# Window attention, conv mixer: score passes in two head halves with the relative bias in spare rows, key blocks placed by GpSimd's DMAs

## The chip, the cores and the metric

The kernel runs on one core of a Trainium2 chip, float32 in and out. The metric is the device time of one launch in microseconds (us), the median over several runs. A core has TensorE (PE, with its weight loads shown as PEld), VectorE (DVE), ScalarE (ACT), GpSimd (POOL) and SyncE (SP), which run side by side and meet at semaphores. PSUM is the memory that TensorE writes to.

## The reference, cut to what matters

Eight images of 64 channels and 32x32 pixels pass through an attention block with its MLP, and then through a block of gated depthwise convolutions. The change is in the attention block only. What that computes:

```python
xn = layernorm(xc)                       # over the 64 channels of each pixel
win = xn in windows of 8x8               # 64 tokens of 64 channels, 8 heads of depth 8
qkv = win @ w_qkv + b_qkv
attn = einsum('bnhd,bmhd->bhnm', q * 8 ** -0.5, k)
bias = rel_bias_table[REL_IDX.reshape(-1)].reshape(64, 64, 8)
attn = softmax(attn + bias.transpose(2, 0, 1)[None], axis=-1)
out = einsum('bhnm,bmhd->bnhd', attn, v) @ w_proj + b_proj
xc = xc + out
h = gelu(layernorm(xc) @ w_mlp1 + b_mlp1) @ w_mlp2 + b_mlp2
xc = xc + h
```

## The kernel before, in words

**Layout.** The 128 partitions hold two images at a time (a batch half `bh` of 64 channels each), and the columns hold four such pairs. The 4096 columns are worked off in NG = 8 groups of G = 512 columns. A group has NW = 8 windows of T = 64 tokens for each of its two images, and 8 heads.

**One window's scores.** A score matrix has 128 rows (64 keys of each of two images) and 512 columns (8 heads by 64 queries). All heads are had from one matrix product over 128 rows of contraction, because one of its two operands is block sparse. `q_heads` and `k_heads` have, for head h, only the rows of that head filled (every eighth row), and `k_blocks` and `q_blocks` have the two images on the diagonal. These operands are put in place by DMAs from `k_parts` and `q_parts`, with the unused places zeroed once at the start. The arithmetic is in float32r, a shortened float32, so the values are split in a high and a low part: for the true scores the product is taken three times (high by high, high by low, low by high).

**The passes.** For each window there is first a maximum pass, from high parts only (`scores_for_max`: one product and one more, `reverse` by `rel`, that adds the relative bias, both 512 columns wide), whose row maxima VectorE takes (`take_maximum`, line 1090). Once a group's eight windows have their maxima, TensorE transposes them (`transpose_maxima`) and VectorE spreads them negated into `minus_max`. The true score pass (`scores`) then has five products of 512 columns: three for the scores (line 778), one for the bias (780) and one, `pick` by `minus_max`, that takes the maximum off (781). ScalarE takes the exponentials (`exponentials`, line 544) into `probs`; TensorE multiplies by the values and by ones (`weighted_values`, `sums`), and VectorE divides (`divide_by_sums`).

**The order of the work.** Each engine has its own `step` for group g, written out by hand, and three later or earlier groups are worked on beside it: `nxt` = g+1 has its maximum pass, `far` = g+2 its layer norm, keys and queries, and `prev` = g-1 its projection, residual and second layer norm. TensorE's step is `scores` 0 to 4 with small work between them, `weighted_values` and `sums` of the first four windows, then the maximum passes in pairs between `scores` 5, 6 and 7, then `keys(far)`, `transpose_maxima(nxt)`, `queries(far)`, and `weighted_values` and `sums` of the other four. The steps of groups 2 to 3 run in a hardware loop on each engine, the others are written out. PSUM has three banks for the maximum pass and two for `scores`, so a maximum pass of window w waits for the reduction of window w-3, and `scores` of window w for the exponential of w-2.

**The waits around the change.** `keys(far)` waits until six of the eight reductions are done. On ScalarE the step ends with `evacuate_k`, `evacuate_q` and `high_of_x` of group g+3, which GpSimd waits for to make the low part (line 284, `low_of_x`), which TensorE waits for in `centered` of the next step. SP's queue holds all DMAs that place operands: `spread_keys` (8 DMAs to `k_heads`, one for each head) and, for each half of the windows, `spread_parts`, which first waits until `scores` of the group before no longer needs the place, then issues 2 DMAs to `k_blocks` and 8 to `q_heads`. GpSimd issues none.

**The start.** `split_bias` makes the bias operand `rel` on VectorE before the first group's `normalise`. GpSimd zeroes `q_blocks`, `k_blocks` and `q_heads`, VectorE `k_heads`.

## Time and profile before

| | us |
|---|---|
| median of 3 runs | 366.39 (365.82 to 370.71) |
| the profiled execution, its own time | 365.95 |
| its span in the trace | 364.1 |
| PE busy | 325.0 (89%) |
| PE weight loads busy | 224.4 (62%) |
| DVE busy | 231.9 (64%) |
| ACT busy | 215.5 (59%) |
| POOL busy | 71.4 (20%) |

The span is the time from the first to the last instruction; the time outside it is 1.85 us here. Busy times of PE are modelled from pipelined instructions: a 512 column product is shown as about 0.39 us long, while the next one starts 0.23 us after it, so starts are compared and not durations. In the chain that ended last, 76% is PE and 11% DVE. The attention steps lie between 36 and 209 us, the MLP after them to about 260, the convolutions to the end.

### The profile page before, as it was taken

The page shows a single profiled execution, that of the slowest core. Times are in us where ns is not written, and L with a number is a line of the kernel's source. Part 1 is how long each engine was busy: PE and PEld are TensorE (multiplying, and loading weights), DVE is VectorE, ACT ScalarE, POOL GpSimd, SP SyncE. Part 2 cuts the span into 40 slices and gives each one's busy share as a digit, 9 for nine tenths or more (in the row PEclk, how much of TensorE's full clock was granted, in tenths as well). Part 3 has the DMA queues.
Part 4 walks back from the last instruction along what each step waited for, and adds up shares of the span by engine and source line. Part 5 has one row for each costly group of instructions (what it writes and reads, how often), then busy time and mean ns, then how long its engine had stood idle before and what let it go on. Part 6 is the DMA issues. An engine that isn't in the chain of part 4 may idle for free.

```text
span 364.1 us, 6376 instructions
## 1 busy us (share of the span) xinstructions
PE 325.0 (89%) x2432; PEld 224.4 (62%) x2432; DVE 231.9 (64%) x376; ACT 215.5 (59%) x350; POOL 71.4 (20%) x63
## 2 busy tenths in 40 slices
PE   2567999999999999999998995999629999999994
PEld 1344676767767677676776753444127777777773
DVE  6557176386783866847758374446976799867411
ACT  6252826668476684765733587989586347646600
POOL 5371101212212122121020391123410000000000
PEclk9989999999999999999999998999959999999999
DMA  7523363322233212332132000076000657788721
GB/s 177 123 61 72 90 126 68 70 56 50 53 66 68 53 49 59 64 70 53 49 63 59 2 0 2 1 147 153 0 2 1 139 121 141 149 166 173 152 61 29
DMA packets 31147, 27.64 MB, mean 76 GB/s; under 512 B 21008, under 2 KB 27664, under 8 KB 31120
## 3 DMA queue, kind: packets, MB, share of 16 engines
q1 hardware_dynamic: 30544, 26.48, 34.6%
q10 hardware_dynamic: 576, 0.79, 0.8%
q8 instruction: 18, 0.29, 0.4%
q14 instruction: 9, 0.07, 0.1%
HBM read 3.78 MB, written 2.10 MB: 16 GB/s over the span
## 4 chain that ended last, share of the span: by engine, by line
PE 76%; DVE 11%; ACT 5%; DMA 3%; SPq 2%; issue 1%; POOL 1%; DVEq 0%; ACTq 0%
PE psum L1007 24%; PE psum L778 11%; PE psum L794 4%; PE psum L759 4%; PE psum L710 4%; PE psum L780 4%; PE psum L781 4%; PE psum L760 4%; PE psum L803 4%; DVE maxima L1090 3%; PE psum L923 3%; DMA probs<-in_rel_table 2%; PE psum L934 2%; PE psum L737 2%; PE psum L811 2%; PE psum L742 1%
## 5 line engine op out<-in xcount | busy, mean ns | idle before, releaser
L1007 PE MATMUL psum<-shifted,conv_w 128*128 128x512 f32 x336 | 87.4, 423 | 9.5 <-ACT conv_w L270 9.5
L1007 PEld LDWEIGHTS psum<-shifted,conv_w 128*128 128x128 f32 x336 | 65.0, 195 | 31.1 <-issue 10.3
L544 ACT ACTIVATE probs<-psum 128x512 f32<-128x512 f32 x64 | 38.3, 598 | 50.1 <-PE psum L781 49.3
L778 PE MATMUL psum<-q_heads,k_blocks 128*128 128x512 f32 x192 | 59.1, 416 | 0.0
L1090 DVE TENSOR_REDUCE maxima<-psum 128x8 f32<-128x512 f32 x64 | 41.1, 685 | 23.7 <-PE psum L760 23.7
L778 PEld LDWEIGHTS psum<-q_heads,k_blocks 128*128 128x128 f32 x192 | 34.9, 188 | 13.6 <-issue 7.1
L284 POOL TENSOR_TENSOR parts<-x,parts 128x256 fp32r<-128x256 f32 (+1 forms) x21 | 19.0, 919 | 102.1 <-ACT parts L493 57.2
L710 PE MATMUL psum<-parts,center_average 128*128 128x512 f32 x64 | 22.7, 438 | 13.7 <-DVE parts L284 12.5
L759 PE MATMUL psum<-k_heads,q_blocks 128*128 128x512 f32 x64 | 27.2, 425 | 4.7 <-DMA k_heads<-k_parts 3.3
L270 ACT CAST conv_w<-conv_w 32x896 fp32r<-32x896 f32 x32 | 30.0, 938 | 0.4
L1104 DVE RECIPROCAL inv_sum<-psum 128x256 f32<-128x256 f32 x16 | 28.0, 1749 | 3.3 <-PE psum L803 3.2
L284 POOL TENSOR_TENSOR parts<-square_logvar,parts 128x512 fp32r<-128x512 f32 x14 | 18.1, 1290 | 53.7 <-ACT square_logvar L557 27.4
L1314 DVE SCALAR_TENSOR_TENSOR x<-psum,weights,x 64x512 f32<-64x512 f32 x16 | 12.0, 750 | 23.3 <-PE psum L1007 23.1
L760 PE MATMUL psum<-rel,reverse 128*128 128x512 f32 x64 | 25.8, 403 | 0.0
L780 PE MATMUL psum<-rel,reverse 128*128 128x512 f32 x64 | 25.1, 393 | 0.0
L781 PE MATMUL psum<-minus_max,pick 128*128 128x512 f32 x64 | 25.0, 391 | 0.0
L662 ACT CAST conv_w<-whole_w 128x896 fp32r<-128x896 f32 x8 | 7.5, 941 | 27.6 <-DVE whole_w L1299 14.9
L710 PEld LDWEIGHTS psum<-parts,center_average 128*128 128x128 f32 x64 | 11.9, 204 | 18.8 <-issue 7.2
L794 PEld LDWEIGHTS psum<-probs,v_blocks 128*32 128x32 f32 x1024 | 15.0, 110 | 8.0 <-issue 8.0
L923 PE MATMUL psum<-normed,mlp_w 128*128 128x512 f32 (+1 forms) x64 | 19.9, 452 | 0.0
L759 PEld LDWEIGHTS psum<-k_heads,q_blocks 128*128 128x128 f32 x64 | 12.5, 196 | 11.4 <-issue 6.6
L630 ACT ACTIVATE hidden<-psum,mlp_bias 128x512 f32<-128x512 f32 x32 | 19.4, 698 | 0.0
(138 smaller groups left out, 516.6 us busy)
## 6 DMA issues: line engine op xcount, KB each, us to landing
shifted<-images SPq DMA_DIRECT2D x32, 332.5 KB, 5.5
k_blocks<-k_parts SPq DMA_DIRECT2D x32, 128.0 KB, 2.8
q_heads<-q_parts SPq DMA_DIRECT2D x128, 32.0 KB, 1.9
k_heads<-k_parts SPq DMA_DIRECT2D x64, 32.0 KB, 1.8
out<-x SPq DMA_DIRECT2D x8, 256.0 KB, 4.8
x<-in_x SPq DMA_DIRECT2D x6, 256.0 KB, 5.9
x<-in_x SPq DMA_DIRECT2D x4, 128.0 KB, 4.7
weights<-in_weights ACTq DMA_DIRECT2D x1, 443.0 KB, 7.9
```

The source lines that it names most:

```text
L270: ins = copy(conv_w[bh][shift * KS:(shift + 1) * KS, part, :, C:], w[(shift - 1) * KS:shift * KS, :, 0:C])
L284: return engine.tensor_tensor(low, whole, high.bitcast(F32), ALU.subtract)
L544: act.activation(probs[:, w, :], psum[:, PROB0 + w % 2, :], ACT.Exp).then_inc(S["ac_probs"], 1)
L710: ins = pe.matmul(psum[:, bank, :], center_average[:, which, :], parts[:, part, :], start=part == 0, stop=part == 1)
L759: pe.matmul(max_bank(w), q_blocks[:, w, :], k_heads[:, :, w * T:(w + 1) * T], start=True, stop=False)
L760: pe.matmul(max_bank(w), reverse[:], rel[:, 0, :], start=False, stop=True).then_inc(S["pe_max"], 1)
L778: pe.matmul(bank, k_blocks[:, w // (NW // 2), k_part, w % (NW // 2), :], q_heads[:, q_part, :, w * T:(w + 1) * T], start=k_part + q_part = ...
L780: pe.matmul(bank, reverse[:], rel[:, 1, :], start=False, stop=False)
L781: pe.matmul(bank, pick[:, w, :], minus_max[:, :, :], start=False, stop=True).then_inc(S["pe_scores"], 1)
L923: ins = pe.matmul(psum[:, HIDDEN0 + m, :], mlp1_w[:, part, f * 128:(f + 1) * 128], normed2[:, bh, bass.ds(n * G, G)], start=part == 0, sto ...
L1007: ins = pe.matmul(psum[:, CONV0 + bh, :], conv_w[bh][:, w_part, t, :], img[:, y:y + H - 1:2, x0:x0 + W], start=t == 0 and w_part + part == ...
L1090: dve.tensor_reduce(maxima[:, w * NH:(w + 1) * NH], max_bank(w).rearrange("p (h t) -> p h t", t=T), AX.X, ALU.max).then_inc(S["dv_max"], 1)
```

## The change: what it does

Heads are grouped in two halves of four, and the 64 channels are laid out so that the heads 0 to 3 of both images fill partitions 0 to 63 and the heads 4 to 7 partitions 64 to 127 (a new order of the weight columns on the host). A product for one head half then needs only 64 of the 128 rows. The other 64 rows carry the relative bias: on one side they hold the reversal matrix, on the other the bias of that head half, so that one product gives scores and bias. Each score product of 512 columns becomes two of 256, one for each head half, and the separate bias products are gone. `k_blocks` and `q_blocks` get one more dimension for the head half. The bias rows are written once, at the start, and the DMAs that place new keys and queries never touch them.

The first place is TensorE, between the end of the first `weighted_values` and `scores(g, 6)` of a step: maximum passes of windows 0 to 3, `scores(g, 5)` and `centered2`. Before:

```order
L759 MATMUL psum<-k_heads,q_blocks 128x512
L760 MATMUL psum<-rel,reverse 128x512
L778 MATMUL psum<-q_heads,k_blocks 128x512 x3
L780 MATMUL psum<-rel,reverse 128x512
L781 MATMUL psum<-minus_max,pick 128x512
```

and with the change:

```order
L823 MATMUL psum<-k_heads,q_blocks 128x256 x4
L842 MATMUL psum<-minus_max,pick 128x512
L845 MATMUL psum<-q_heads,k_blocks 128x256 x6
L823 MATMUL psum<-k_heads,q_blocks 128x256 x4
L773 MATMUL psum<-parts,center_average 128x512 x2
```

A window's maximum pass goes from two instructions of 512 columns to two of 256 (the rows of before show one window's pair, those of now two windows at a time), and a window's `scores` from five of 512 to one of 512 and six of 256.

The second place is the end of ScalarE's step. Before:

```order
L514 ACTIVATE k_parts<-psum,qkv_bias 128x2x256
L521 ACTIVATE q_parts<-psum,q_bias 128x2x256
L529 CAST q_blocks<-q_parts 64x8x64 x2
L493 CAST parts<-x 128x256 x2
```

and with the change:

```order
L561 ACTIVATE k_parts<-psum,qkv_bias 128x2x256
L568 ACTIVATE q_parts<-psum,q_bias 128x2x256
L577 CAST q_blocks<-q_parts 32x8x64 x4
L541 CAST parts<-x 128x256 x2
```

Each batch half was one copy of 64 partitions; each pair of head half and batch half is now one of 32 partitions and as many columns.

The third place is GpSimd's step, where the DMAs to `k_blocks` now stand:

```order
L285 TENSOR_TENSOR parts<-square_logvar,parts 128x512 [waits ac_sq]
L285 TENSOR_TENSOR parts<-x,parts 128x512 [waits ac_x1]
L285 TENSOR_TENSOR parts<-square_logvar,parts 128x512 [waits ac_sq2]
L450 DMA k_blocks<-k_parts 32x16x64 [waits dv_k_low,pe_scores]
L450 DMA k_blocks<-k_parts 32x16x64 x3
L285 TENSOR_TENSOR parts<-x,parts 128x256 [waits x_high]
```

Four DMAs, each for 32 partitions and both window halves, stand before the low part of x; they wait for all eight `scores` of the group before, and `scores(g, 0)` waits for all four of them.

The core of the diff:

```diff
         def _(pool):
+            def spread_key_blocks(n, par):
+                if isinstance(n, int) and n == 0:
+                    pool.wait_ge(S["k_blocks_zeroed"], 1)
+                    pool.wait_ge(S["k_blocks_set"], 1)
+                else:
+                    pool.wait_ge(S["pe_scores"], NW * n)
+                pool.wait_ge(S["dv_k_low"], n + 1)
+                for hh in range(2):
+                    for bh in range(2):
+                        r = slice(hh * 64 + bh * 32, hh * 64 + bh * 32 + 32)
+                        pool.dma_start(k_blocks[r, hh, :, :, :, bh * T:(bh + 1) * T]..., k_parts[r, par]...
+                                       ).then_inc(S["k_blocks_in"], 16)
...
+                if nxt is not None:
+                    spread_key_blocks(nxt, 1 - par)
                 if after is not None:
                     low_of_next_x(after)
+            pool.wait_ge(S["dv_rel_flipped"], 1)
+            pool.tensor_scalar(key_rows(0), bias_rows(rel_flipped, 0, range(NW)), not_in_half(0), None, ALU.mult)...
             low_of_next_x(1)
-            pool.memset(q_heads[:].bitcast(F32), 0.0).then_inc(S["zeroed"], 1)
+            spread_key_blocks(0, 0)
+            late = range(NW // 2, NW)
+            for half in range(2):
+                pool.tensor_scalar(query_rows(0, half, late), bias_rows(rel_high, half, late), not_in_half(half), None, ALU.mult)
             low_of_next_square(1)
+            for half in range(2):
+                ins = pool.tensor_scalar(query_rows(1, half, late), bias_rows(rel_low, half, late), not_in_half(half), None, ALU.mult)
             low_of_next_x(2)
...
         ScalarE, evacuate_q
-                for bh in range(2):
-                    r = slice(bh * C, (bh + 1) * C)
-                    ins = act.copy(q_blocks[r, :, bh * T:(bh + 1) * T]..., q_parts[r, par, :, 0, :]...)
+                for hh in range(2):
+                    for bh in range(2):
+                        r = slice(hh * 64 + bh * 32, hh * 64 + bh * 32 + 32)
+                        ins = act.copy(q_blocks[r, hh, :, bh * T:(bh + 1) * T]..., q_parts[r, par, :, 0, :]...)
         ScalarE, the start
+            for half in range(2):
+                ins = act.activation(k_blocks[:, half, :, 0], reversal()..., ACT.Copy, scale=not_in_half(half))
...
+            for half in range(2):
+                act.activation(query_rows(0, half, early), bias_rows(rel_high, half, early), ACT.Copy, scale=not_in_half(half))
             evacuate_k(0, 0)
             evacuate_q(0, 0)
+            for half in range(2):
+                ins = act.activation(query_rows(1, half, early), bias_rows(rel_low, half, early), ACT.Copy, scale=not_in_half(half))
...
         TensorE, scores_for_max and scores
-                pe.matmul(max_bank(w), q_blocks[:, w, :], k_heads[:, :, w * T:(w + 1) * T], start=True, stop=False)
-                pe.matmul(max_bank(w), reverse[:], rel[:, 0, :], start=False, stop=True).then_inc(S["pe_max"], 1)
+                for hh in range(2):
+                    ins = pe.matmul(max_bank(w)[:, hh * G // 2:(hh + 1) * G // 2], q_blocks[:, hh, w, :],
+                                    of_half(k_heads, hh)[:, :, w * T:(w + 1) * T], start=True, stop=True)
+                ins.then_inc(S["pe_max"], 1)
...
+                if w == 0:
+                    pe.wait_ge(S["k_blocks_in"], 64 * (g + 1))
...
-                for k_part, q_part in ((0, 0), (0, 1), (1, 0)):
-                    pe.matmul(bank, k_blocks[:, w // (NW // 2), k_part, w % (NW // 2), :], q_heads[:, q_part, :, w * T:(w + 1) * T], ...)
-                pe.matmul(bank, reverse[:], rel[:, 1, :], start=False, stop=False)
-                pe.matmul(bank, pick[:, w, :], minus_max[:, :, :], start=False, stop=True).then_inc(S["pe_scores"], 1)
+                pe.matmul(bank, pick[:, w, :], minus_max[:, :, :], start=True, stop=False)
+                for hh in range(2):
+                    for k_part, q_part in ((0, 0), (0, 1), (1, 0)):
+                        ins = pe.matmul(bank[:, hh * G // 2:(hh + 1) * G // 2], k_blocks[:, hh, w // (NW // 2), k_part, w % (NW // 2), :],
+                                        of_half(q_heads[:, q_part], hh)[:, :, w * T:(w + 1) * T], ...)
+                ins.then_inc(S["pe_scores"], 1)
...
         VectorE, the start
+            for half in range(2):
+                ins = dve.tensor_scalar(q_blocks[:, half], reversal(), not_in_half(half), None, ALU.mult)
...
-            split_bias()
+            bias_with_keys()
             normalise(0)
+            low_of_bias()
```

`bias_with_keys` copies the flipped bias table into `rel_flipped` (two copies of 64 partitions) and fills the bias rows of `k_heads` for one head half (2048 columns); `low_of_bias` makes `rel_low` with two subtractions. SP's `spread_parts` becomes `spread_queries`, with its 8 DMAs to `q_heads` alone, which for the first group wait for the bias rows (`q_heads_set0`, `q_heads_set1`).

## Rows read from the trace of the kernel before

**Rows 1.** The page: busy time of each engine, and clock granted to TensorE.

```profile
PE 325.0 (89%) x2432; PEld 224.4 (62%) x2432; DVE 231.9 (64%) x376; ACT 215.5 (59%) x350; POOL 71.4 (20%) x63
...
PEclk9989999999999999999999998999959999999999
```

**Rows 2.** Stretches of time: one whole step, the last but one, the last.

```profile
105.42:128.56 23.14, 23.08 (x242) 16.55 (x241) 15.88 (x26) 15.09 (x29) 5.28 (x5) 1.00 0.27 58
174.90:196.00 21.10, 20.19 (x233) 15.19 (x233) 13.99 (x23) 9.83 (x19) 2.58 (x2) 1.00 0.28 61
...
196.00:216.00 20.00, 19.72 (x223) 14.19 (x224) 11.98 (x15) 13.06 (x22) 9.56 (x8) 1.00 0.04 9
```

**Rows 3.** Timeline of PE: start, length, line, count, idle time before.

```profile
115.98 0.50 PE L759 MATMUL psum<-k_heads,q_blocks 128*128 128x512 f32 x1
...
120.44 0.39 PE L781 MATMUL psum<-minus_max,pick 128*128 128x512 f32 x1
120.67 0.39 PE L759 MATMUL psum<-k_heads,q_blocks 128*128 128x512 f32 x1
...
125.54 1.13 PE L737 MATMUL psum<-normed,qkv_w 128*128 128x512 f32 x2
126.59 1.10 PE L794 MATMUL psum<-probs,v_blocks 128*32 128x64 f32 x64
...
128.49 0.97 PE L778 MATMUL psum<-q_heads,k_blocks 128*128 128x512 f32 x3
...
129.75 1.05 PE L742 MATMUL psum<-qkv_w,normed 128*128 128x128 f32 x8
130.56 0.93 PE L778 MATMUL psum<-q_heads,k_blocks 128*128 128x512 f32 x3
...
131.80 0.62 PE L710 MATMUL psum<-parts,center_average 128*128 128x512 f32 x2
...
139.11 0.50 PE L759 MATMUL psum<-k_heads,q_blocks 128*128 128x512 f32 x1
```

**Rows 4.** All of one line and form: count, busy us, mean ns.

```profile
L778 PEld LDWEIGHTS psum<-q_heads,k_blocks 128*128 128x128 f32 x192 | 34.9, 188 | 13.6 <-issue 7.1 <-ACT probs L544 0.4
...
L406 POOL TENSOR_TENSOR pick<-consts 128x1024 fp32r<-128x1024 f32 x1 | 2.0, 2030 | 3.7 <-DMA consts<-in_consts 3.7
```

**Rows 5.** Timeline of DVE in the same step.

```profile
119.41 1.75 DVE L1104 RECIPROCAL inv_sum<-psum 128x256 f32<-128x256 f32 x1
...
121.53 1.88 DVE L1090 TENSOR_REDUCE maxima<-psum 128x8 f32<-128x512 f32 x3
123.83 1.29 DVE L1090 TENSOR_REDUCE maxima<-psum 128x8 f32<-128x512 f32 x2 [0.42 <-PE psum L760]
```

**Rows 6.** Timeline of ACT, the end of the step and the start of the next.

```profile
126.70 0.69 ACT L521 ACTIVATE q_parts<-psum,q_bias 128x512 fp32r<-128x512 f32 x1 [0.86 <-DMA q_heads<-q_parts]
127.42 1.25 ACT L529 CAST q_blocks<-q_parts 64x512 fp32r<-64x512 f32 x2
128.69 0.71 ACT L493 CAST parts<-x 128x256 fp32r<-128x256 f32 x2
```

**Rows 7.** Timeline of POOL, one step earlier.

```profile
106.35 1.41 POOL L284 TENSOR_TENSOR parts<-x,parts 128x256 fp32r<-128x256 f32 x2 [7.30 <-ACT parts L493]
110.93 1.29 POOL L284 TENSOR_TENSOR parts<-square_logvar,parts 128x512 fp32r<-128x512 f32 x1 [3.17 <-ACT square_logvar L499]
```

**Rows 8.** SP's queue over the end of that step; DMA issues of the page.

```profile
122.90 1.30 SPq L356 DMA_DIRECT2D k_blocks<-k_parts  x2
124.25 5.98 SPq L362 DMA_DIRECT2D q_heads<-q_parts  x8
...
k_blocks<-k_parts SPq DMA_DIRECT2D x32, 128.0 KB, 2.8
```

**Rows 9.** Timelines of the start: ACT, DVE and PE.

```profile
21.90 1.54 ACT L539 COPY v_blocks<-psum 64x256 f32<-64x256 f32 x4
23.46 0.60 ACT L498 ACTIVATE parts<-psum 128x512 fp32r<-128x512 f32 x1
...
30.82 0.69 DVE L1076 TENSOR_TENSOR normed<-psum,rstd 128x512 f32<-128x512 f32 x1 [1.15 <-ACT rstd L506]
...
35.97 1.03 PE L778 MATMUL psum<-q_heads,k_blocks 128*128 128x512 f32 x3
```

More of the change, by code:

```diff
@@ L303, in halves, with patches, of_half, not_in_half @@
             return t.rearrange("p (s c) -> p s c", s=2)
-        ZERO_Q_BLOCKS, ZERO_Q_HEADS, NZERO = 1, 4, 5
+        NZERO = 2
+        def patches(n):
+            return rel_raw[:, n, :, :].rearrange("p (a b) h -> p h a b", a=WS)[:, :, :, 0:WS]
+        def of_half(t, half):
+            return t[:, half * (NH // 2):(half + 1) * (NH // 2), :]
+        def not_in_half(half):
+            a = _AT["not_in_half"][0] + half
+            return consts[:, a:a + 1]
+        def reversal():
+            return const("reverse").unsqueeze(1).to_broadcast([128, NW, 128])
+        def bias_rows(rel, half, windows):
+            rel = of_half(rel.bitcast(F32).rearrange("p (h t) -> p h t", h=NH), half)
+            return rel.unsqueeze(2).to_broadcast([128, NH // 2, len(windows), T])
+        def key_rows(half):
+            return of_half(k_heads, half).rearrange("p h (w t) -> p h w t", t=T)
+        def query_rows(part, half, windows):
+            rows = of_half(q_heads[:, part], half).rearrange("p h (w t) -> p h w t", t=T)
+            return rows[:, :, windows.start:windows.stop, :]
         block = ctx.enter_context(nc.Block())
@@ L365, in _ @@
             spread_keys(0)
[L366 to L367 removed]
+            spread_queries(0, 0)
+            spread_queries(0, 1)
             spread_keys(1)
@@ L371, in _ @@
             for g in range(NG - 1):
-                for half in range(2):
-                    spread_parts(g + 1, half)
+                spread_queries(g + 1, 0)
+                spread_queries(g + 1, 1)
                 if g + 2 < NG:
@@ L401, in _ @@
         def _(pool):
-            for t in (q_blocks[:].bitcast(F32), k_blocks[:].bitcast(F32), gaps[:]):
-                pool.memset(t, 0.0).then_inc(S["zeroed"], 1)
+            pool.memset(k_blocks[:, :, :, 1].bitcast(F32).rearrange("p h s w t -> p (h s) (w t)"), 0.0).then_inc(S["k_blocks_zeroed"], 1)
+            pool.memset(gaps[:], 0.0).then_inc(S["zeroed"], 1)
             pool.wait_ge(S["consts_in"], 16)
@@ L603, in _ @@
             evacuate_q(0, 0)
+            act.wait_ge(S["dv_rel_low"], 1)
+            for half in range(2):
+                ins = act.activation(query_rows(1, half, early), bias_rows(rel_low, half, early), ACT.Copy, scale=not_in_half(half))
+            ins.then_inc(S["q_heads_set0"], 1)
             act.wait_ge(S["v_zeroed"], 1)
@@ L1039, in _ @@
             dve.tensor_scalar(qkv_w[:, 1:3, :], qkv_raw[:, 1:3, :], vec[:, 0:1], None, ALU.mult)
+            dve.wait_ge(S["consts_in"], 16)
+            for half in range(2):
+                ins = dve.tensor_scalar(q_blocks[:, half], reversal(), not_in_half(half), None, ALU.mult)
+            ins.then_inc(S["q_blocks_set"], 1)
             dve.wait_ge(S["pe_qkv_bias"], 1)
```

123 lines of the change are left out of this document (62 added, 61 removed).

## The prediction

> **What bounds the kernel now.** I read the page first. TensorE is busy for 89% of the span, nobody else for more than 64%, and its clock is at full speed (2.4 GHz) from the second slice to where attention ends [rows 1]. The stretches by step say more: in a whole attention step of 23.14 us TensorE is busy for 23.08, VectorE for 15.9, ScalarE for 15.1, GpSimd for 5.3 [rows 2]. So a step lasts as long as TensorE's instructions; counted back from group 6, which begins at 174.9, five such steps (groups 1 to 5) fill the time from 59 us on. The timeline of PE gives the price of one: a product of 512 columns takes 0.23 us from start to start (120.44 to 120.67) [rows 3]. The timelines of the other engines then show how far behind TensorE they are, which decides what a shorter TensorE step is worth.
>
> **TensorE's own share.** A step removes 16 instructions of 512 columns (8 in the maximum pass, 8 in `scores`), 3.7 us, and cuts the 32 other products with `k_heads`, `q_blocks`, `k_blocks` and `q_heads` from one of 512 to two of 256. Of the latter the trace has none in this form. Below half of 0.23 they can't be (0.114, as many columns in all); at the other end, if a weight load (0.188 us each [rows 4]) could not run under the product before it, it is 0.19. But the eight 128-column instructions of `values` take 0.81 us (129.75 to 130.56), 0.10 each, with a full 128x128 weight load before each [rows 3], so loads do run under products and keep that pace. I take 0.118. A window's `scores` then takes 0.23 + 6 x 0.118 = 0.94 us against 1.15, its maximum pass 0.24 against 0.46: per step 8 x 0.21 + 8 x 0.22 = 3.45 us less. If nothing else mattered, a step would last 19.7 us.
>
> **What is late next.** I walk one step of the changed kernel, with time 0 at its first maximum pass (115.98 in the trace, the next at 139.11 [rows 3]).
>
> 1. VectorE. Window 2's maximum pass comes after two others and one `scores`: 0.47 + 0.94 + 0.4 = 1.8 us. A reduction takes 0.61 (1.88 for three), `divide_by_sums` 2.12 (119.41 to 121.53) [rows 5]. So the third reduction ends at 2.45, the division at 4.57, and the other five at 7.7. In the kernel before, they end at 9.1 (125.12), with 0.42 us of idle time: VectorE is nearly the limit there already. TensorE, with three banks and `keys` waiting for the sixth reduction, loses about 0.9 us.
> 2. TensorE: transpose 0.36, `queries` 1.05 (125.54 to 126.59) [rows 3]: ends at 9.15, against 10.6 before.
> 3. ScalarE: `q_parts` 0.72, then the copies to `q_blocks`. Two took 1.25 [rows 6]. There are now four, and although each has half the partitions it has as many columns, so I keep 0.62 each: 2.5 us. `high_of_x` 0.71: ends at 13.2, against 13.4 before (129.40). Of the 1.4 us won so far only 0.2 are left.
> 4. GpSimd: low part of x, 1.41 [rows 7]: 14.7, and by the same sum 14.9 before.
> 5. TensorE's `centered` can start at 14.75. In the kernel before it starts at 15.8 (131.80) [rows 3], 0.9 after its data was there; now TensorE is through with the second values and sums (1.9, 126.59 to 128.49) at 11.05 and gets to `centered` two `scores` and the values later, at 11.05 + 0.94 + 0.81 + 0.94 = 13.75, and waits 1.0.
> 6. From there TensorE takes `centered` 0.46, `scores` 2 and 3 with the projection 2.7, a wait of about 0.25 for GpSimd's low square (1.29 [rows 7], after ScalarE's square, which stands behind an exponential and the four copies of v), variance 0.5, `scores` 4 0.94, values and sums 1.9: the step ends at 21.5.
>
> So **a step lasts 21.5 us** against 23.13: 1.6 of the 3.45 us are had, since the chain of reductions, queries, copies, low part and `centered` closes on itself. Five steps: 8.0 us.
>
> **Group 6** has no x to come. Its first part is TensorE's: 10.62 (128.49 to 139.11) less `centered` and variance (1.0) and 5 x 0.21, 8.6 us. The second part ends when `k_blocks` is there, 11.15 after its start (below). Together 19.7 against 21.1 [rows 2]: 1.4 less. **Group 7** has no maximum pass, and TensorE is busy throughout (19.72 of 20.0 us, the start of the MLP among them) [rows 2]: 8 x 0.21 = 1.7 less.
>
> **The start.** The bias rows cost VectorE two fills of `q_blocks`, GpSimd 2048 columns of `k_heads` and 4096 of `q_heads` in place of a memset of 8192, ScalarE two fills of `k_blocks` and four of `q_heads`. Most of it lies under waits for the first loads and for keys. What doesn't: between `q_parts` and `evacuate_v` ScalarE has two more copies (1.25) and two fills of 1024 columns, twice a 512-column instruction at 0.5 us from start to start. `evacuate_v` moves from 21.90 to 25.1, the square behind it from 23.46 to 26.7 [rows 9], and by way of GpSimd the `normalise` of group 1 from 30.82 to about 31.3: 0.5 us. In the first step the four copies stand before the first exponential, another 1.2; the shorter second part gives 1.0 back, and the passes of group 0 the rest. Net 0.25 later, with bounds of 0 and 4 (if GpSimd takes 2 us for each DMA, its low square is 4 us late).
>
> **GpSimd's DMAs.** SP took 0.65 us to issue one to `k_blocks` (1.30 for two), and 2.8 us from issue to landing [rows 8]. GpSimd issues none in this trace. From below I bound it by SP's 0.65; from above by the slowest instruction that GpSimd has in steady work, 2.03 us for 1024 columns [rows 4], about two columns for each 256-byte run of such a DMA. The nearest row in kind is SP's, the nearest in engine is the other, and I take 1.0. The four are issued once `scores(g, 7)` is done, at 5.0 in the walk, so the last lands at 5.0 + 4x + 2.15 = 7.15 + 4x us: 11.15 for x = 1.0. TensorE is ready for `scores(g+1, 0)` at 11.05, and 1.0 more cost nothing, because it then waits for x anyway. So in the five steps the DMAs are free up to x = 1.2. The cover is that wait: were `centered` ready earlier, they would be the limit. The queue behind them on GpSimd, the low part of x, is needed from 13.2 on, so it is held up only above x = 2.0. SP's queue gets 2.6 us a step shorter: after `scores(g, 7)` it has 5.98 for `q_heads` and, at that pace, no more for the 8 of `k_heads`, which with 2 us to land are there by 19, 2.5 us before they are needed. I cost that at nothing.
>
> The Trainium skill has a price (DMA: Bandwidth & Descriptors, Latency and other measured facts): the first byte of a DMA from GpSimd comes after about 1 us, from SP after 0.6. Added once to SP's pace, as an estimate, the last would land at 10.2 and the sum would stay; the same page (SWDGE vs HWDGE vs iDMA) says that GpSimd writes every descriptor in software, which speaks against this change, and no run here shows it yet.
>
> **Sum.** 365.95 + 0.25 - 8.0 - 1.4 - 1.7 = **355 us**. The profiled execution lies 0.4 below the median of 366.39, so the two can be held for one.
>
> **Rivals.**
>
> *A. GpSimd's DMAs become the limit (slower).* Place: `scores(g+1, 0)` waits for the last of four, where only the first half's two DMAs, issued four windows earlier, were waited for before. Each step is 7.15 + 4x - 12.05 longer, for groups 0 to 5, and the start of group 7's `scores`, with no wait for x behind it, slips by 7.15 + 4x - 11.15. It eats the whole gain at x = 1.6 (landing at 13.5), makes the kernel 2% slower at x = 1.85, and at the upper bound of 2.03 gives 355 + 6 x 3.2 + 4.1 = 378.5. For it: GpSimd takes 1.29 us where VectorE takes 0.69 for the same kind of work, and each DMA has 512 runs of 256 bytes. Against it: nothing of GpSimd's 15 idle us a step is needed for other work, and 512 KB is 3 to 4 us for the DMA engines, which are busy for 0.27 of the step [rows 2]. Chance 0.38 for x above 1.33, where the time is no longer 2% below: 0.14 for within 2%, 0.24 for slower.
>
> *B. TensorE stays the limit.* If the four copies are quicker for having half the partitions, or reductions overlap better, the chain falls under TensorE's 19.7 us. Then 5 x 1.8 = 9 less: 346. For it: TensorE's waits in my chain, 0.9 for reductions, 1.0 and 0.25 for GpSimd, are small sums of many rows. Against: each step of it is a measured row. Chance 0.10.
>
> *C. Pairs of 256 columns go at the pace of weight loads, 0.19.* `scores` takes 1.37, a maximum pass 0.38, a step 23.1 + 8 x 0.22 - 8 x 0.08 = 24.2, and the kernel 366 + 8 = 374. The row of `values` speaks against it. Chance 0.03.
>
> My forecast, 350 to 359, has 0.45, and 0.04 remains for a start that costs up to 4 us more (359 to 362). Two per cent, about what a measurement of this kernel can tell from no change, is 7.3 us: faster means below 359.1. That is the forecast and B, 0.55; within 2% 0.18; slower, A above x = 1.85 and C, 0.27. The range goes from B's 346 to A's upper bound of 379; the forecast's own is 350 to 359.
>
> **What the profile after would show.** First maximum pass to first maximum pass of 21.5 us in groups 2 to 5, with PE busy for about 19.7; products of 256 columns 0.12 apart; an idle time of PE before `centered`, ended by GpSimd's low part of x, of about 0.9 us, and before `keys` or the transpose, ended by a reduction; four copies to `q_blocks` of 0.62 each. If the idle time stands before `scores(g, 0)` and a DMA ended it, A holds, and the time from issue to landing gives x. If there is none before `centered`, B does. The forecast is wrong most of all if one DMA from GpSimd takes more than 1.3 us.

## The result, and the profile after

| | before | changed |
|---|---|---|
| median, us | 366.41 (365.82 to 370.71) | 373.37 (370.6 to 374.99) |
| ratio | | 1.0169 [1.0106, 1.0232] |
| profiled execution: its time, span | 365.95, 364.1 | 372.76, 371.0 |

The changed kernel is about 7 us slower where 11 us less were forecast; 373.4 lies in the range given. Whether it is more than 2% slower the interval leaves open, but not that it is slower. On another chip, on which both kernels were measured again, it was 372.55 against 369.97, a ratio of 1.0077 [1.004, 1.0113]. By these two ratios it costs 1 to 2%. They differ by the kernel before: its single executions took under 367 us in three of four on the first chip and in 2 of 44 on the others, where nearly all took 368 to 372.

From the page of the changed kernel (busy time, clock of TensorE, two DMA issues):

```profile
PE 311.6 (84%) x2560; PEld 222.4 (60%) x2560; DVE 237.4 (64%) x377; ACT 232.7 (63%) x374; POOL 102.1 (28%) x98
...
PEclk9966889999999999999987995999968999999999
...
k_blocks<-k_parts POOLq DMA_DIRECT2D x32, 128.0 KB, 4.1
...
k_heads<-k_parts SPq DMA_DIRECT2D x64, 32.0 KB, 1.8
```

Against [rows 1], TensorE has 13 us less to do and idles more; its granted clock is lower from 19 to 56 us and near 200 us. A DMA to `k_blocks` takes 4.1 us from issue to landing, where SP's, issued two at a time, took 2.8 [rows 8]. The waits of TensorE, by what ended them (total, times, longest):

```profile
PE psum L773 <- DVE parts L285: 15.2, 4, 5.9
...
PE psum L842 <- DMA k_blocks<-k_parts: 8.0, 7, 2.5
PE psum L823 <- DMA k_heads<-k_parts: 7.2, 1, 7.2
```

In the kernel before, the first kind came to 12.5 us, the second to nothing and the third to 3.3. To see when they cost time I cut both spans at the same events of PE's timelines (first `scores` of groups 1, 6 and 7, first product of the MLP, first of the convolutions). Microseconds of each stretch, and the forecast's term for it:

| stretch | before | changed | difference | forecast |
|---|---|---|---|---|
| to `scores(1, 0)` | 59.09 | 64.41 | +5.3 | +0.25 |
| five steps, to `scores(6, 0)` | 115.70 | 111.37 | -4.3 | -8.0 |
| to `scores(7, 0)` | 21.11 | 22.76 | +1.7 | -1.4 |
| to the MLP | 15.72 | 15.96 | +0.2 | -1.7 |
| to the convolutions | 59.22 | 62.95 | +3.7 | 0 |
| to the end | 93.3 | 93.5 | +0.2 | 0 |

No term of attention is right in full. One step of the changed kernel, from group 3's first maximum pass, on PE:

```profile
97.11 0.74 PE L823 MATMUL psum<-k_heads,q_blocks 128*128 128x256 f32 x4
...
105.30 1.12 PE L800 MATMUL psum<-normed,qkv_w 128*128 128x512 f32 x2
106.36 1.10 PE L860 MATMUL psum<-probs,v_blocks 128*32 128x64 f32 x64
...
108.96 0.47 PE L842 MATMUL psum<-minus_max,pick 128*128 128x512 f32 x1 [0.65 <-DMA k_blocks<-k_parts]
109.27 0.87 PE L845 MATMUL psum<-q_heads,k_blocks 128*128 128x256 f32 x6
109.98 1.05 PE L805 MATMUL psum<-qkv_w,normed 128*128 128x128 f32 x8
...
112.15 0.74 PE L773 MATMUL psum<-parts,center_average 128*128 128x512 f32 x2 [0.18 <-POOL parts L285]
...
119.13 0.62 PE L823 MATMUL psum<-k_heads,q_blocks 128*128 128x256 f32 x3
```

and ScalarE and GpSimd beside it:

```profile
107.18 2.50 ACT L577 CAST q_blocks<-q_parts 32x512 fp32r<-32x512 f32 x4
109.71 0.71 ACT L541 CAST parts<-x 128x256 fp32r<-128x256 f32 x2
```

```profile
102.41 2.57 POOL L450 DMA_DIRECT2D k_blocks<-k_parts  x4 [0.19 <-issue]
110.50 1.60 POOL L285 TENSOR_TENSOR parts<-x,parts 128x256 fp32r<-128x256 f32 x2 [5.52 <-ACT parts L541]
```

This is the walk of the prediction: queries done at 9.25 (forecast 9.15), high x at 13.3 (13.2), `centered` at 15.0 (14.75), six products of 256 columns in 0.71 us, 0.119 apart (0.118). Only the landing is off: GpSimd issues a DMA in 0.65 us, and `scores` can start at 11.85, where TensorE was ready at 11.2. In the next step it starts at 12.4, and the wait is 1.1. Of the four DMAs of a group the first lands 3.0 us after its issue and the last, the one that counts, 4.4 to 5.2.

### The profile page after: what moved, and what is told of

It is laid out like the page before. It is cut to its first block, busy times and chain, and to the rows that moved or that the text cites. A ratio compares the mean times of both kernels' runs of the same rounds, so it can differ in the third digit from the quotient of the medians.

```text
span 371.0 us, 6661 instructions
## 1 busy us (share of the span) xinstructions
PE 311.6 (84%) x2560; PEld 222.4 (60%) x2560; DVE 237.4 (64%) x377; ACT 232.7 (63%) x374; POOL 102.1 (28%) x98
## 2 busy tenths in 40 slices
DMA packets 15788, 27.66 MB, mean 75 GB/s; under 512 B 4624, under 2 KB 11280, under 8 KB 15760
## 3 DMA queue, kind: packets, MB, share of 16 engines
q1 hardware_dynamic: 13648, 22.29, 26.6%
q0 software_dynamic: 1536, 4.20, 6.9%
## 4 chain that ended last, share of the span: by engine, by line
PE 45%; POOL 13%; ACT 11%; issue 10%; DMA 9%; DVE 9%; SPq 1%; DVEq 0%; POOLq 0%; ACTq 0%
PE psum L1072 24%; DMA k_blocks<-k_parts 7%; POOL parts L285 6%; PE psum L845 5%; POOL k_blocks L450 4%; PE psum L988 3%; PE psum L773 3%; DMA x<-in_x 2%; PE psum L842 2%; PE psum L999 2%; ACT v_blocks L587 2%; DVE normed L1195 2%; POOL q_heads L472 2%; POOL q_heads L476 2%; ACT probs L592 1%
## 5 line engine op out<-in xcount | busy, mean ns | idle before, releaser
L845 PEld LDWEIGHTS psum<-q_heads,k_blocks 128*128 128x128 f32 x384 | 56.6, 196 | 5.6 <-issue 1.8
L845 PE MATMUL psum<-q_heads,k_blocks 128*128 128x256 f32 x384 | 57.7, 287 | 0.0
L773 PE MATMUL psum<-parts,center_average 128*128 128x512 f32 x64 | 25.2, 479 | 19.9 <-DVE parts L285 15.2
L842 PE MATMUL psum<-minus_max,pick 128*128 128x512 f32 x64 | 30.5, 477 | 9.6 <-DMA k_blocks<-k_parts 8.0
L823 PE MATMUL psum<-k_heads,q_blocks 128*128 128x256 f32 x128 | 24.1, 311 | 9.9 <-DMA k_heads<-k_parts 7.2
L823 PEld LDWEIGHTS psum<-k_heads,q_blocks 128*128 128x128 f32 x128 | 19.7, 204 | 15.3 <-issue 10.5
L1382 DVE SCALAR_TENSOR_TENSOR x<-psum,weights,x 64x512 f32<-64x512 f32 x16 | 12.0, 750 | 23.3 <-PE psum L1072 23.1
L450 POOL DMA_DIRECT2D k_blocks<-k_parts x32 | 20.8, 657 | 15.0 <-PE psum L845 8.9
L501 POOL TENSOR_TENSOR images<-square_logvar,images 128x512 f32 (+1 forms) x8 | 10.3, 1289 | 46.1 <-ACT images L707 46.1
L842 PEld LDWEIGHTS psum<-minus_max,pick 128*128 128x128 f32 x64 | 12.5, 195 | 17.2 <-issue 13.9
L577 ACT CAST q_blocks<-q_parts 32x512 fp32r<-32x512 f32 x32 | 19.7, 616 | 0.5
```

The source lines that it names most:

```text
L450: pool.dma_start(k_blocks[r, hh, :, :, :, bh * T:(bh + 1) * T].bitcast(F32).rearrange("p s l w t -> p (s l w) t"), k_parts[r, par].bitcast ...
L773: ins = pe.matmul(psum[:, bank, :], center_average[:, which, :], parts[:, part, :], start=part == 0, stop=part == 1)
L823: ins = pe.matmul(max_bank(w)[:, hh * G // 2:(hh + 1) * G // 2], q_blocks[:, hh, w, :], of_half(k_heads, hh)[:, :, w * T:(w + 1) * T], sta ...
L842: pe.matmul(bank, pick[:, w, :], minus_max[:, :, :], start=True, stop=False)
L845: ins = pe.matmul(bank[:, hh * G // 2:(hh + 1) * G // 2], k_blocks[:, hh, w // (NW // 2), k_part, w % (NW // 2), :], of_half(q_heads[:, q_ ...
```

## The experiments

Each ratio is to runs of the kernel before on the same chip. Its medians there were 370.0 to 370.5 us, 4 us above the 366.4 of the first chip, so ratios are compared, and times only between traces. Dots mark what is left out of a diff; semaphore counts that an edit makes necessary are left out too.

**SP issues the key blocks** (all 32, between the two query halves).

```diff
 GpSimd, step
-                if nxt is not None:
-                    spread_key_blocks(nxt, 1 - par)
 SP, for each group
                 spread_queries(g + 1, 0)
+                spread_key_blocks(g + 1, (g + 1) % 2)
                 spread_queries(g + 1, 1)
```

> The changed kernel, with the DMAs to k_blocks issued by SP again (four a group, between the two halves of the queries' DMAs, after the same wait), nothing else changed. Theory A (GpSimd's DMAs cost time in every step and in the last one): SP's issue takes 0.65 us like GpSimd's, but they land 2.8 us after issue and not 4.1, so the wait for k_blocks before scores(g, 0), 0.65 to 1.2 us a step in the changed kernel, goes, and the 2.5 us before group 7 with its gap of 4.15 us in front of the 32nd DMA go too: steps of about 21.8 us for 22.3, s(7) 3 us earlier, and the kernel about 367 to 368. Theory B (the loss is at the start and the chain through ScalarE and GpSimd closes at 22 us anyway): steps stay at 22.0 to 22.3 and the kernel above 370.

364.01 us (363.42 to 364.27), ratio 0.9811 [0.9764, 0.9859], 3 us under what either theory gave. This undoes one of the change's two parts, and the other is a gain. By stretch: 63.05, 108.95, 19.79, 14.45, 62.42, 93.3. Of the 9.0 us less than the changed kernel's span, 2.4 are in the five steps, 3.0 in group 6, 1.5 in group 7, 1.4 in the start. In the steps, what ends TensorE's waits now is what the walk named, and the blocks are waited for once, ahead of group 7:

```profile
PE psum L773 <- POOL parts L285: 7.1, 14, 1.1
...
PE psum L842 <- DMA k_blocks<-k_parts: 0.6, 1, 0.6
```

**Group 0's blocks from SP, the other 28 from GpSimd.**

```diff
 GpSimd, start
-            spread_key_blocks(0, 0)
 SP, start
             spread_keys(0)
+            spread_key_blocks(0, 0)
             spread_queries(0, 0)
```

> The changed kernel with group 0's four key-block DMAs issued by SP and the other 28 by GpSimd. Theory of the shared start: in the changed kernel the k_heads DMAs took 3.3 us to land beside GpSimd's k_blocks DMAs (1.8 before), so the first max pass began at 27.66 instead of 25.44; here it begins near 25.7, as when SP issued all blocks (25.65). Theory of a full ring: GpSimd's 32nd DMA stalled 4.15 us because of how many it had issued; with 28 there is no such stall, and group 7's first scores come about 11.5 us after its max pass begins instead of 14.2. Together the time is 2 to 5 us under the changed kernel's 373.4. Rival: the stall belongs to that place in the program (GpSimd held by something else near 190 us) and stays at 4 us whatever the count; and the late start comes from the fills on GpSimd, so the first max pass stays at 27.7. Then the time is within 1 us of 373.4.

369.18 us (365.61 to 372.07), ratio 0.9946 [0.9903, 0.9989]. Both theories, of the shared start and of the full ring, hold in what they said of the trace. In the changed kernel the first key DMAs share the time from 19 to 25 us with GpSimd's, and the issues in the stretch from 17 to 30 us (count, size, us to landing) read

```profile
k_blocks<-k_parts POOLq DMA_DIRECT2D x4, 128.0 KB, 4.1
k_heads<-k_parts SPq DMA_DIRECT2D x8, 32.0 KB, 3.3
```

and in this one

```profile
k_blocks<-k_parts SPq DMA_DIRECT2D x4, 128.0 KB, 3.3
k_heads<-k_parts SPq DMA_DIRECT2D x8, 32.0 KB, 1.8
```

so its first maximum pass starts at 25.89 instead of 27.66 (25.44 before). The second view also gives SP's price for four of these DMAs in a row, 3.3 us and not the 2.8 of two; the page of the version with x first, below, has 3.3 as well. And GpSimd isn't held in group 6. The changed kernel's GpSimd there:

```profile
189.61 1.93 POOL L450 DMA_DIRECT2D k_blocks<-k_parts  x3 [0.19 <-issue]
195.69 0.66 POOL L450 DMA_DIRECT2D k_blocks<-k_parts  x1 [4.15 <-issue]
```

this one's:

```profile
189.07 2.58 POOL L466 DMA_DIRECT2D k_blocks<-k_parts  x4 [0.18 <-issue]
```

The five steps stay at 111.1. And of the 1.8 us won at the first maximum pass only 0.3 are left at `scores(1, 0)` (64.11), which now waits 2.2 us for group 1's blocks: GpSimd issued them from 55.52 on, and the last landed at 63.9, 6.2 us after its issue. Why so long there, no run tells.

**Four more DMAs** (group 1's issued a second time, 36 in all; one run).

```diff
 GpSimd, step, after spread_key_blocks(nxt, 1 - par)
+                    if isinstance(nxt, int) and nxt == 1:
+                        pool.wait_ge(S["k_blocks_in"], 128)
+                        spread_key_blocks(nxt, 1 - par)
```

> The changed kernel with the four key-block DMAs of group 1 issued a second time by GpSimd (the same data to the same place), 36 in all instead of 32. Theory of a full ring: what holds GpSimd is the count of its DMAs, so the hold of 4 us moves one group forward, ahead of the fourth DMA of group 6 (near 172 us, the 32nd issued), and the fourth of group 7 has none or one of its own. Rival: it belongs to group 7's place in the program, and stays ahead of the fourth DMA of group 7 alone, near 196 us. In both the first scores of group 1 come some 4 us later.

383.12 us, one run, with `scores(1, 0)` at 71.23. The hold moved one group forward, with its count:

```profile
155.25 2.57 POOL L450 DMA_DIRECT2D k_blocks<-k_parts  x4 [0.18 <-issue]
177.43 1.93 POOL L450 DMA_DIRECT2D k_blocks<-k_parts  x3 [0.19 <-issue]
183.56 0.66 POOL L450 DMA_DIRECT2D k_blocks<-k_parts  x1 [4.19 <-issue]
201.75 2.57 POOL L450 DMA_DIRECT2D k_blocks<-k_parts  x4 [0.21 <-issue]
```

28 DMAs stand ahead of the group at 177.43, so the held one is again the 32nd. It is the count, not the place. The traces also show when the hold ends: the 31st DMA lands at 182.88 and GpSimd issues the 32nd at 183.56; in the changed kernel it lands at 195.01 and the issue is at 195.69. So GpSimd seems to wait here until its earlier DMAs have landed. What it is that is full after 31 such DMAs is not shown.

**The kernel before with GpSimd issuing its key blocks** (after all eight `scores`, as in the changed kernel).

```diff
 SP, spread_parts
-                    sp.dma_start(k_blocks[r, half, ...
 GpSimd, step
+                if nxt is not None:
+                    spread_key_blocks(nxt, 1 - par)
```

> The kernel before, with only the DMAs to k_blocks moved to GpSimd: its four DMAs of a group are issued after all eight scores of the group before, where SP had issued the first half's two after four of them. Scores in one piece, bias products kept. Theory A: in the kernel before, 5.7 us lie between the last scores of a group and the first of the next; four issues of 0.65 and 4.1 us to land from the last one take 6.1, so each step waits 0.5 to 1 us, the 32nd DMA is held up as in the changed kernel (2 us more before group 7), and the kernel takes 370 to 374. Theory B: the DMAs from GpSimd are slow only beside the changed kernel's other DMAs: steps stay at 23.1 and the kernel at 366 to 368.

370.86 us (368.86 to 373.46), ratio 1.0043 [1.0, 1.0086]. The wait in each step that theory A named did not come. With the long score passes the DMAs hide: TensorE waits for `k_blocks` once, 0.5 us, and the five steps take 115.9. The page has 3.7 us to landing, and the 32nd DMA is held there too (3.03 us, until 0.01 us after the 31st landed). So in the five steps the same move costs next to nothing where a step is 23.1 us long, and 2.4 us where it could be 21.8.

The trace is 4.2 us longer than that of the kernel before, and 3.5 of them lie in the stretch from the MLP to the convolutions (62.73 for 59.22), which this edit doesn't touch. The next run is about that stretch.

**Memsets later.** When the last scores are done, GpSimd zeroes the padded images with eight memsets, beside VectorE's casts for the MLP.

```diff
 GpSimd, after the last scores
             pool.wait_ge(S["pe_scores"], NW * NG)
+            pool.wait_ge(S["dv_high2"], NG - 1)
             for b4 in range(NB4):
                 for part in range(2):
                     ins = pool.memset(images[:, part, b4, :].bitcast(F32), 0.0)
```

> The changed kernel, with GpSimd's memsets of the images held back until VectorE has made the high part of group 6's second norm. Theory 1 (two casts of 64x512 on VectorE take 5.88 us for 0.86 since GpSimd's memsets run beside them): the casts take 0.9 us, the residual of group 7 comes 5 us earlier, and the kernel is 3 to 5 us shorter, unless the casts of group 7 then meet the memsets in turn (up to 3 us back). Theory 2 (the casts are long for another reason): they stay near 2.9 us each, and the kernel is the same or later.

367.69 us (366.47 to 373.49), ratio 0.9908 [0.987, 0.9945], 1.7 to 2.6% less than the two ratios of the changed kernel. VectorE and GpSimd in the changed kernel:

```profile
216.83 5.88 DVE L1195 CAST normed<-rstd 64x512 fp32r<-64x512 f32 x2
```

```profile
211.83 10.01 POOL L493 MEMSET images<- 128x1444 f32 x8
221.78 0.21 POOL L496 MEMSET small<- 128x128 f32 x1
```

and with the memsets behind the casts:

```profile
218.14 0.85 DVE L1196 CAST normed<-rstd 64x512 fp32r<-64x512 f32 x2
```

The casts of 5.88 us end 0.7 after the last memset in all nine traces that have them, whenever the memsets start. One of the two took 5.44 us, the other 0.42. In the kernel before, the two took 3.08: VectorE got in between two memsets, twice. It is not the changed kernel's timing that takes this from it. The kernel before (first two lines) and the same with GpSimd's DMAs (last two) have

```profile
213.95 3.08 DVE L1128 CAST normed<-rstd 64x512 fp32r<-64x512 f32 x2
208.94 10.58 POOL L445 MEMSET images<- 128x1444 f32 x8
214.48 5.88 DVE L1138 CAST normed<-rstd 64x512 fp32r<-64x512 f32 x2
209.48 10.02 POOL L455 MEMSET images<- 128x1444 f32 x8
```

In both, and in the changed kernel, the casts start 5.00 us after the first memset and 0.02 to 0.03 after the fifth. So the long casts come with the unchanged attention code too, at the same place in the memsets, and which of the two happens is not explained by the change; what decides it is not shown. The Trainium skill (SBUF — State Buffer, SBUF: two separate sides) says that VectorE, in its two-port modes, and GpSimd lock a shared port pair for a whole instruction, and that the loser is blocked. The trace agrees that one of the two waits; but a memset is 1.25 us, and the cast stood behind four of them, not one.

With the memsets late, the stretch to the convolutions is 56.25 us, against 62.95 in the changed kernel and 59.22 in the kernel before.

**The kernel before with only the borders zeroed.**

```diff
-                    ins = pool.memset(images[:, part, b4, :].bitcast(F32), 0.0)
+                    img = images[:, part, b4, :].bitcast(F32)
+                    pool.memset(img[:, 0:PAD * PW + PAD], 0.0)
+                    a = PAD * PW + PAD + W
+                    pool.memset(img[:, a:a + (H - 1) * PW].rearrange("p (y x) -> p y x", x=PW)[:, :, 0:2 * PAD], 0.0)
+                    ins = pool.memset(img[:, a + (H - 1) * PW:], 0.0)
```

> The kernel before with only the borders of the padded images zeroed by GpSimd instead of the whole of them (the insides are overwritten anyway). Theory that the memsets hold VectorE: in the kernel before the two casts of the MLP's normed weights took 3.08 us at 213.95, in the changed one 5.88, and in the one with the memsets later 0.85; so the kernel before too loses some 2 to 5 us there, and with short memsets the casts take 0.9 us and the time falls by 2 to 6 us, to 361 to 368. Rival: the cast's length in the kernel before is set by something else on VectorE (other operands' transfers), and the casts stay near 3 us and the time within 1 us of before.

366.56 us (364.87 to 367.34), ratio 0.9881 [0.9824, 0.9938]. The casts take 0.85 us. Yet the profiled execution's stretch to the convolutions is 59.02, as before: the next products of the MLP start 1.5 us earlier (222.82 instead of 224.35), but at a granted clock of 0.66 in 220 to 230 us where before has 0.83, and that gives it back. The medians differ by 1.2%, 3.9 us, all the same. The one trace of the kernel before is of an execution of 365.95 us, 4 us under its median on this chip. That most of its executions there have casts of 5.88 us, worth 3.5 us, would account for the difference, and the run with GpSimd's DMAs (370.1 us, casts of 5.88) speaks for it; none of the executions of 370 us of the kernel before itself was traced, so it stays likely and not shown.

**Bias fills on VectorE**, all five that GpSimd had.

```diff
 GpSimd, start
-            pool.tensor_scalar(key_rows(0), bias_rows(rel_flipped, 0, range(NW)), not_in_half(0), None, ALU.mult)
...
-                pool.tensor_scalar(query_rows(0, half, late), bias_rows(rel_high, half, late), not_in_half(half), None, ALU.mult)
...
 VectorE, start
+                dve.tensor_scalar(query_rows(0, half, late), bias_rows(rel_high, half, late), not_in_half(half), None, ALU.mult)
...
```

> The changed kernel, with GpSimd's bias fills of the start (2048 columns of k_heads, 4 x 1024 of q_heads) done by VectorE. Theory 1 (GpSimd's fills, 17.8 us of its time for 6144 columns, push its low square and low x back, TensorE then idles and runs at the lower clock until 56 us): the fills take VectorE 1.3 us for 2048 columns, the first scores start near 36.5 us for 39.2, the first maximum pass of group 1 near 48.5 for 52.1, the kernel 3 to 4 us shorter, near 369.5. Theory 2 (the start is late for k_heads' DMAs, which land at 27.6 for 25.4 because of the DMAs to k_blocks beside them): first scores at 38 or later, less than 1.5 us won.

372.44 us (370.54 to 375.18), ratio 1.0052 [1.0015, 1.0089]: nothing. The 2048 columns of `k_heads` take 1.28 us there instead of GpSimd's 6.53, and the first maximum pass is at 27.71 all the same, since it waits for the `k_heads` DMAs (above). GpSimd's long fills are not the late start.

**Busy TensorE at the start** (with SP issuing): ten products of 512 columns in the first wait and one beside each window of the first maximum pass; nothing reads them.

```diff
 TensorE, start
             centered(1)
+            pe.wait_ge(S["po_pick"], 1)
+            for i in range(10):
+                pe.matmul(psum[:, PROB0, :], pick[:, 0, :], pick[:, 0:4, :], start=True, stop=True)
             for w in range(NW):
                 scores_for_max(0, w)
+                pe.matmul(psum[:, PROB0, :], pick[:, 0, :], pick[:, 0:4, :], start=True, stop=True)
```

> The changed kernel with SP issuing the key blocks, and TensorE given products that nothing reads at the start: ten of 512 columns while it waits for the first k_heads, and one beside each of the eight windows of the first max pass (where the kernel before had its bias products). Theory of the clock: the start lost 4.8 us at the first max pass of group 1 (47.08 before, 51.91 with SP issuing) because TensorE idled for 4.6 us and did half the products of before in the stretch from 19 to 37 us, where its granted clock was 0.72 and 0.50 (before 0.84 and 0.97); with more work there the clock in 28 to 37 us is above 0.9, that max pass begins at 47 to 49, and the time is 2 to 4 us under the 364.0 without them. Rival: the start is late by the chains of ScalarE and VectorE with their fills (q_blocks copies as four, bias fills), the added products only delay, and the time is 364 to 366.

363.73 us (362.33 to 367.78), ratio 0.9799 [0.9745, 0.9854], the same as without. The traced execution is the one of 367.78; its extra time lies in group 6 (23.4 us for 19.8), behind the stretches read here. The windows of 28 to 37 us (length, busy PE, PEld, DVE, ACT, POOL, clock), without and with the products:

```profile
28.00:37.00 9.00, 6.08 (x15) 3.93 (x16) 5.14 (x10) 1.96 (x5) 7.40 (x5) 0.50 0.25 62
```

```profile
28.00:37.00 9.00, 6.59 (x27) 4.75 (x27) 6.19 (x12) 2.13 (x6) 8.30 (x5) 0.86 0.35 74
```

The granted clock went from 0.50 (1.2 GHz throughout) to 0.86, and group 1's first maximum pass only from 51.91 to 51.81. The clock had been low where TensorE had little to do, and it didn't make the start late. My theory was wrong.

**ScalarE: the high part of x ahead of the four copies** (with SP issuing).

```diff
 ScalarE, evacuate_q
+                if x_ahead is not None:
+                    high_of_x(x_ahead)
                 act.wait_ge(S["ac_q_high"], n + 1)
...
-                if after is not None:
-                    high_of_x(after)
```

> The changed kernel with SP issuing the key blocks, and ScalarE taking the high part of the next x before its four copies to q_blocks instead of behind them. Theory: with the key blocks back on SP a step of 21.5 us ends with the centring of the next group waiting for ScalarE's chain (q_parts, four copies of 0.62 us, high part of x, GpSimd's low part); putting x first brings GpSimd's low part forward by 2.5 us, and a step gets 0.3 to 1 us shorter, 2 to 6 us in all. Rival: the copies themselves, which the next max pass and its DMAs wait for, are on the path, or TensorE is now the limit; the time is then 363 to 366, the same.

362.4 us (361.72 to 362.62), ratio 0.977 [0.9722, 0.9818]; SP's blocks alone had 0.9811, so the intervals overlap, and the trace tells more: a span of 360.8 against 362.0. The step goes from 21.8 to 21.6, and `scores(1, 0)` from 63.05 to 61.55: the chain over the four copies is part of the late start. In the step most of the wait only moves, from `centered` (0.85 us with SP's blocks alone) to the variance, which needs GpSimd's low square:

```profile
155.15 0.73 PE L773 MATMUL psum<-parts,center_average 128*128 128x512 f32 x2 [0.71 <-POOL parts L285]
```

**The versions that put these together:** SP issuing, x first, and memsets late or cut to the borders. They ran with the changed kernel itself on one chip.

> Three edits together on the changed kernel: SP issues the key blocks, ScalarE takes the high part of the next x first, and GpSimd's memsets of the images wait for the seventh of VectorE's subtractions of normed's high part, so that they don't lie beside its casts. If the three costs are separate, the 362.4 us of the first two falls by what the late memsets gave alone (373.4 to 367.7, 5.7 us, of which some may be chance), to 356 to 359; the two casts take 0.9 us instead of 5.88. Rival: TensorE, which then runs on from the last group into the MLP, finds something else late (VectorE's or ScalarE's chain of the LayerNorm) or a lower granted clock, and the time stays within 2 us of 362.4.

> The same three with the memsets cut to the borders of the images instead of put off. With the kernel before that shortened the casts to 0.85 us but TensorE's clock was 0.66 in 220 to 230 us and gave back 1.5 us. Theory: the same as with late memsets, 356 to 359, since the casts are free in both. Rival: the short memsets leave the casts free but the granted clock falls behind them as it did there, and it is 1 to 2 us slower than with late memsets.

> The changed kernel itself on the chip on which the others of this call run, as their measure: 370 to 375 us, a ratio of 1.00 to 1.02 to the kernel before; its five steps 21.9 to 22.3 us, its GpSimd held about 4 us ahead of its 32nd key-block DMA, its casts beside the memsets 5.9 us.

Memsets late: 356.88 us (355.12 to 359.9), ratio 0.9669 [0.9617, 0.9722]. Borders: 358.59 (357.15 to 360.39), 0.9694 [0.9645, 0.9744]. The changed kernel: 372.55 (371.41 to 375.23), 1.0077 [1.004, 1.0113]. So the head halves with three edits are 3.3% faster than the kernel before. In the traces the gains add: late memsets take 6.9 us from the stretch to the convolutions here and 6.7 alone. But the memsets are no cost of the change, since shorter ones make the kernel before 1.2% faster too; borders against borders (0.9694 and 0.9881), the head halves with SP's blocks and x first are worth 1.9%. By stretch the first has 60.67, 107.95, 19.80, 15.47, 56.10, 93.3. The intervals of borders and late overlap, though the profile has the borders' stretch to the convolutions at 58.97, with a clock of 0.77 in 205 to 220 us against

```profile
205.00:220.00 15.00, 12.34 (x48) 6.45 (x47) 9.30 (x16) 13.80 (x22) 10.43 (x9) 1.00 0.01 2
```

in the other.

## Why the prediction was wrong

- **"Net 0.25 later, with bounds of 0 and 4"** was wrong, by the most: +5.3 us. Of these, 2.2 are there at the first maximum pass, and 1.8 of them come from GpSimd's four DMAs beside the `k_heads` ones. "I cost that at nothing", said of SP's shorter queue, looked at the queue and not at the DMA engines behind it. From there to `scores(1, 0)` it was 33.65 us before and 36.75 in the changed kernel. With blocks from SP that stretch takes 37.40, with x first as well 35.92: ScalarE's chain over four copies, which I had on the path for 0.5, is worth 1.5 there. For the last 2.3 us I have no run; the clock at 28 to 37 us and GpSimd's fills have no part in them.
- **"Five steps: 8.0 us"** brought 4.3. The walk itself holds: with blocks from SP the five steps give 6.7, and each point of it is within 0.3 us of the forecast; the chain closes at 21.8 and not 21.5, which makes 1.3 of the missing 3.7. What failed, for the other 2.4, is "I take 1.0" with "the last lands at 11.15". The issue costs 0.65 us, the lower bound, but the last of four lands 4.4 to 5.2 us after its issue and not 2.8. I had carried the landing over from SP as if only the issue could differ, and from pairs of DMAs to fours: SP's own fours take 3.3. So `scores` started 11.85 to 12.4 us into the step, as if x were 1.2 to 1.3, just where the prediction's cover (up to 1.2) ends. The mechanism was rival A's, at a small price. The cover was real: in the step shown the blocks' wait of 0.65 us came out of the wait before `centered`, 0.18 there and 0.85 with SP's blocks. The estimate from the Trainium skill, 10.2, was further off.
- **"Group 6 ... 1.4 less"** became 1.7 more. With SP it is 1.3 less, so the term was right; the hold of the 32nd DMA (4.15 us, of which 2.47 reached TensorE) and a clock of 0.72 around it took it. No row of before could show a limit on a queue that it doesn't use, and "from above by the slowest instruction" bounded each DMA and not their number.
- **"Group 7 ... 1.7 less"**: 0.2 more. It began at a granted clock of 0.72, behind the hold; in the first two kernels without a hold it is 14.45 and 14.46 us, 1.3 less than before (with x first, 14.84 to 15.47).

```profile
192.00:204.00 12.00, 9.39 (x106) 7.22 (x107) 6.12 (x11) 1.79 (x3) 0.66 (x1) 0.72 0.25 51
```

- **The MLP had no term**, and +3.7 us was measured in its stretch. The casts were blocked for 5.0 us behind the memsets, and TensorE's longest wait for VectorE there grew from 2.36 to 5.16 us. But the kernel before with only its DMAs moved has the same 3.5 us more, with the same start of the casts in the memsets. So this part of the 7 us is probably the luck of the executions of 366 us, the traced one among them, and not a price of the change. Without it the stretches add up to 3.1 us, near the 2.6 us between the medians on the chip where the kernel before took 370. Leaving this term out was then no error.
- Rival C is out: 0.119 us for each product of 256. Rival B is out: no version's step fell below 21.6.

The step that turned the sign is the pricing of the DMAs: issue and landing of one were priced, and not the `k_heads` DMAs beside them at the start, the landing of the last of four, or the number that GpSimd issues in all. The head halves alone end just above the forecast's own range of 350 to 359: the ratio of 0.981 makes 359.5 us of 366.4. The GpSimd part of the change took that and more.

## What to carry to other kernels

When a transfer moves to another engine's queue, price issue and landing apart, ask what else is in flight at the moment, and count how many of them the program issues in all. When a stretch that the change doesn't touch comes out longer, look whether another version of the old kernel has that too before you put it down to the change. And measure the two parts of a change apart: here one was worth -2%, and the other took it and more.

## What the runs showed of the hardware that I had not expected

- A DMA of 128 KB in 512 runs of 256 bytes: 0.65 us to issue on GpSimd as on SP; to landing, in fours, 4.1 us from GpSimd (3.7 in the kernel before) against 3.3 from SP, and 2.8 from SP in pairs. The page of the changed kernel counts 1536 packets in GpSimd's queue, 48 for each DMA; SP's queue has 30544 packets with these DMAs and 13648 without, 528 for each.
- GpSimd stood 3.0 to 4.2 us ahead of its 32nd such DMA, in all six traces that have it, and not with 28; with 36 the four after the 32nd were not held. In the four traces that show the landing of the 31st, the 32nd was issued 0.0 to 0.7 us after it.
- VectorE's cast took 5.44 us beside four GpSimd memsets of 1.25 us each, (in nine traces), and 0.41 without them; in one, with the same start, the two casts took turns with the memsets and needed 3.08 together.
- A fill of 2048 columns: 6.53 us on GpSimd, 1.28 to 1.29 on VectorE.
- A copy of 32 partitions by 512 columns takes ScalarE 0.62 us, the same as one of 64 partitions.
